# A transformer block with routed spline FFN: second layer norm of y moved to ScalarE, output summed in DRAM from beta rows, x2 and scaled y

## The reference

```python
mod = silu(c) @ wmod                       # sa, ca, ga, sb, cb, gb per sequence
h = layernorm(x) * (1 + ca) + sa
x = x + ga * attention(h)                  # q, k, v, |scores| causal softmax, Wo: this sum is x2
h = layernorm(x) * (1 + cb) + sb
# routed FFN on h
tile_idx = best of 64 signatures (cluster of 8, then 8 in it), scores = h @ sigs.T
comp = tanh(gelu(h @ w1 + b1) @ w2 + b2)
mag  = spline of comp with the tables of tile_idx          # one number per row
y = h + mag * directions[tile_idx] * output_scale
y = (y - mean(y)) / sqrt(var(y) + 1e-5) * norm_gamma + norm_beta
out = x + gb * y
```

## Time and profile before

| | us |
|---|---|
| three runs, median (lowest to highest) | 448.58 (447.64 to 449.85) |
| the profiled execution | 450.27 |
| its span, first to last instruction | 448.4 |
| TensorE, VectorE, ScalarE, GpSimd busy | 398.0, 381.2, 305.8, 32.8 |

### The profile page before, as it was taken

One profiled execution on the slowest core, in us unless ns is written; L12 is line 12 of the kernel. 1 busy time (PEld: TensorE's weight loads), 2 busy tenths in 40 slices (PEclk: granted clock), 3 DMA queues, 4 the chain that ended last, 5 costly groups with the idle time before them and its releaser, 6 DMA issues.

```text
span 448.4 us, 7857 instructions
## 1 busy us (share of the span) xinstructions
PE 398.0 (89%) x2107; PEld 309.7 (69%) x2107; DVE 381.2 (85%) x1464; ACT 305.8 (68%) x670; POOL 32.8 (7%) x77
## 2 busy tenths in 40 slices
PE   8999999999999998999999999999999978947120
PEld 8786776886787787786877687768777765736110
DVE  4785548789989988999889888898889999998996
ACT  1435767886998599769983798478956885755420
POOL 4000061000000011000101001010101010001110
PEclk9999999999999999999999999999999999966555
DMA  7723503033003243430428004432314144007153
GB/s 226 233 57 92 144 5 118 0 119 111 8 2 118 95 94 59 131 96 24 72 93 190 24 2 90 136 97 32 62 57 99 20 70 72 1 1 118 27 75 109
DMA packets 32907, 35.66 MB, mean 80 GB/s; under 512 B 3370, under 2 KB 28448, under 8 KB 32864
## 3 DMA queue, kind: packets, MB, share of 16 engines
q1 hardware_dynamic: 25024, 27.15, 19.6%
q0 software_dynamic: 7536, 7.48, 12.1%
q10 hardware_dynamic: 304, 0.54, 0.4%
HBM read 19.36 MB, written 15.79 MB: 78 GB/s over the span
## 4 chain that ended last, share of the span: by engine, by line
PE 78%; DVE 9%; ACT 7%; issue 5%; DMA 1%; DVEq 0%; ACTq 0%
PE bank L610 14%; PE bank L627 13%; PE bank L587 12%; PE bank L600 12%; PE bank L649 7%; PE bank L618 4%; PE bank L636 3%; PE bank L575 3%; PE bank L689 3%; PE bank L680 2%; DVE y L2316 1%; DVE res L2330 1%; ACT gath L1365 1%; DVE y L2293 1%; ACT xhat L1256 1%
## 5 line engine op out<-in xcount | busy, mean ns | idle before, releaser
L627 PE MATMUL bank<-v,probsT 128*128 128x257 f32 x320 | 79.3, 382 | 2.0 <-ACT probsT L1293 0.9
L610 PE MATMUL bank<-h,g 128*128 128x128 f32 (+3 forms) x256 | 78.6, 434 | 0.0
L627 PEld LDWEIGHTS bank<-v,probsT 128*128 128x128 f32 x320 | 58.1, 190 | 14.7 <-issue 3.7
L600 PE MATMUL bank<-m_ga,h 128*128 128x258 f32 x256 | 65.4, 382 | 2.1 <-ACT onehotT L1359 1.6
L587 PE MATMUL bank<-h,a_sb 128*128 128x512 f32 x128 | 60.0, 594 | 0.0
L600 PEld LDWEIGHTS bank<-m_ga,h 128*128 128x128 f32 x256 | 46.2, 190 | 13.5 <-issue 5.1
L610 PEld LDWEIGHTS bank<-h,g 128*128 128x128 f32 x256 | 42.7, 190 | 16.4 <-issue 9.3
L2032 POOL DMA_DIRECT2D out<-res x14 | 17.9, 1280 | 346.8 <-DVE res L2330 255.1
L1282 ACT ACTIVATE bank<-bank,v 128x128 f32<-128x128 f32 (+1 forms) x64 | 31.8, 498 | 15.7 <-PE bank L610 15.5
L1287 ACT ACTIVATE probs<-probs,negmax 128x128 f32<-128x128 f32 (+1 forms) x64 | 35.8, 562 | 6.3 <-DVE negmax L2145 6.0
L1306 ACT ACTIVATE wide<-x,nmr,rstd 128x256 f32<-128x256 f32 x64 | 35.2, 594 | 4.1 <-DVE nmr L2090 4.1
(11 more groups left out here) (183 smaller groups left out, 792.4 us busy)
## 6 DMA issues: line engine op xcount, KB each, us to landing
x<-in_L_attn_x SPq DMA_DIRECT2D x16, 512.0 KB, 3.9
out<-x SPq DMA_DIRECT2D x14, 512.0 KB, 5.0
out<-res POOLq DMA_DIRECT2D x14, 512.0 KB, 6.3
gb_row<-gate_rows SPq DMA_DIRECT2D x16, 256.0 KB, 3.4
a_row<-gate_rows SPq DMA_DIRECT2D x14, 256.0 KB, 3.6
out<-res SPq DMA_DIRECT2D x2, 512.0 KB, 3.5
wide<-in_L_wmod SPq DMA_DIRECT2D x1, 768.0 KB, 8.2
wide<-in_L_wmod ACTq DMA_DIRECT2D x1, 512.0 KB, 5.8
```

The costliest lines, as they stand in the source:

```text
L600: last = mm(ps[:, 0:VW], h[s][:, c, t * P:(t + 1) * P], m_ga[p % 2][s][:, c, :], start=(c == 0), stop=(c == KC - 1))
L610: last = mm(ps[:, 0:w], g[s][:, c, t * P:(t + 1) * P], h[s][:, c, 0:w], start=(c == 0), stop=(c == KC - 1))
L627: last = mm(ps[:, 0:D + 1], probsT[s][t][:, j * P:(j + 1) * P], v_sb[s][:, j, 0:D + 1], start=(j == 0), stop=(j == t))
```

## The change

- The mean of y comes without reading y. `FS` gets one more column of -1/D (FW = 137), so the mean of h arrives with the scores, `table` holds the mean of each direction, and `spl` gets two more small steps that give `nmu3`.
- The variance: ScalarE squares (y + nmu) with a running sum (`y_sq`, 64 of them). `y_st` is gone, `y_var` is one small instruction.
- Groups 0 to 7: ScalarE normalises y (`yh`, 56 tiles), VectorE multiplies by gb*gamma (`yg`, one instruction for `oa` and `ob`).
- out: SyncE first spreads the row gb*beta over a sequence of out (`beta`, from DRAM to DRAM), GpSimd adds x2 (`ax`) and then the scaled y (`ay`), both by accumulating transfers. y has two buffers.
- `ms` and `base` move from VectorE to GpSimd. `ms(p)` for p > 2 and `base(g)` wait for the first y of a group, group p-2 for ms and g for base.
- Groups 8 and 9 keep `oa`, `base` and `ob`; `send` goes out in halves.
- All banks and the orders of all five queues are new.

```diff
-    FW = NCL + NTILES + H
+    MEAN = NCL + NTILES
+    FW = MEAN + 1 + H
...
+        nmu3, guess3 = ([sb(f"{n}_3{q}", [P, PT]) for q in range(2)] for n in ("nmu", "guess"))
+        y = [sb(f"y{q}", [P, PT, D]) for q in range(2)]
...
@@ sync
-            def xo(g, i):
-                spq.wait_ge(x2_rdy, NT * (before(g) + i + 1))
-                spq.dma_start(out_v[GROUPS[g][i]], x2[p % 2][s][:, :, :]).then_inc(x2_sent[p % 2][s], 16)
+            def beta(g, i):
+                p, s = of_group(g, i)
+                if g == 0:
+                    spq.wait_ge(gb_sent, 16)
+                need(spq, x2_sent[p % 2][s], 16 * (p // 2))
+                rows_ = gate_rows[GROUPS[g][i]:GROUPS[g][i] + 1, 3 * D:4 * D]
+                spq.dma_start(out[GROUPS[g][i]], rows_.broadcast_to([S, D])).then_inc(beta_sent[p % 2][s], 16)
...
@@ scalar
+            def y_sq(g, t):
+                n = NT * before(g)
+                act.wait_ge(nmu_rdy, g + 1)
+                act.wait_ge(y_rdy, n + t + 1)
+                need(act, ln3_var, g)
+                A(gath[:, t, PAR:GW], y[g % 2][:, t, :], ACT.Square, bias=nmu3[g % 2][:, t:t + 1],
+                  accum_out=ln3["sq"][:, t:t + 1]).then_inc(sq_rdy, 1)
             def yh(g, t):
                 act.wait_ge(ln3_ready, g + 1)
-                A(y[:, t, :], y[:, t, :], ACT.Identity, bias=ln3["nmr"][:, t:t + 1],
+                own = y[g % 2][:, t, :]
+                A(own, own, ACT.Identity, bias=ln3["nmr"][:, t:t + 1],
                   scale=ln3["rstd"][:, t:t + 1]).then_inc(yhat_rdy, 1)
...
@@ gpsimd
+            def ms(p, s):
...
+                need(pool, v_done, NT * seq(p - 2, s) + NT)
+                if p > 2:
+                    pool.wait_ge(y_rdy, NT * seq(p - 3, 0) + 1)
+                tt(m_ga[p % 2][s][:, :, 0:D], m_sb[:, :, :],
+                   a_row[p % 2][s][:, 0:D].unsqueeze(1).broadcast_to([P, KC, D]), ALU.mult).then_inc(ms_rdy, 1)
+            def base(g, u):
...
+                pool.wait_ge(y_rdy, NT * before(g) + 1)
+                tt(res[:, o:o + 2, :], x2[p % 2][s][:, t, :],
+                   gb_row[g % 2][u // 2][:, 1:2, :].broadcast_to([P, 2, D]), ALU.add).then_inc(base_rdy, 1)
+            def ax(g, i):
+                (p, s) = of_group(g, i)
+                pool.wait_ge(beta_sent[p % 2][s], 16 * (p // 2 + 1))
+                pool.wait_ge(x2_rdy, NT * (before(g) + i + 1))
+                gp.dma_start(out_v[GROUPS[g][i]], x2[p % 2][s][:, :, :], accum_op=ALU.add).then_inc(x2_sent[p % 2][s], 16)
             def ay(g, i):
-                pool.wait_ge(alone_rdy, NT * (before(g) + i + 1))
+                pool.wait_ge(scaled_rdy, NT * (before(g) + i + 1))
...
@@ vector
-            def y_st(g, t):
-                dve_ln3.mark(v.bn_stats(ln3["st"][:, t, :], y[:, t, :]))
             def y_var(g, i):
-                variance(i, dve_ln3, ln3, slice(0, tiles(g)), ln3_var)
+                dve.wait_ge(sq_rdy, NT * before(g + 1))
+                ts(ln3["var"][:, own], ln3["sq"][:, own], 1.0 / D, EPS, ALU.mult, ALU.add).then_inc(ln3_var, 1)
+            def yg(g, t):
+                dve.wait_ge(yhat_rdy, NT * before(g) + t + 1)
+                own = y[g % 2][:, t, :]
+                tt(own, own, gb_row[g % 2][t // NT][:, 0, :], ALU.mult).then_inc(scaled_rdy, 1)
...
             def y_(g, t):
-                need(dve, alone_rdy, min(NT * before(g), NT * before(g - 1) + t + 1))
+                need(dve, summed[g % 2][t // NT], 16 * len(with_slot(range(g % 2, g, 2), t // NT)))
...
```

More of the change, by code:

```diff
@@ L1959, in _ @@
                 c_ga(9, i)
+            y_gs(8)
+            for i in range(0, 4):
+                y_sq(9, i)
             y_gs(9)
@@ L2727, in _ @@
+            b_x2(2, 1, 0)
+            for i in range(3, 8):
+                clc(2, i)
+            b_ttr(2, 1, 3)
+            b_ri(2, 1, 1)
+            b_x2(2, 1, 1)
+            clc(2, 8)
+            y_var(0, 0)
+            y_nw(0, 0)
+            clc(2, 9)
+            a_st(4, 0, 0)
+            b_st(2, 0, 3)
+            y_nw(0, 1)
+            for i in range(0, 5):
+                clb(2, i)
+            y_nw(0, 2)
             pick(2, 0)
-            b_st(2, 0, 2)
+            y_nw(0, 3)
@@ new lines, in _ @@
+            for i in range(2, 4):
+                clc(4, i)
+            a_nw(5, 1)
+            y_nw(2, 1)
+            a_nw(5, 2)
+            clc(4, 4)
+            b_ri(4, 0, 2)
+            a_nw(5, 3)
+            b_v(4, 1, 2)
+            b_x2(4, 0, 2)
+            for i in range(2, 4):
+                y_nw(2, i)
+            clc(4, 5)
+            for i in range(0, 7):
+                spl(3, i)
+            b_ri(4, 0, 3)
+            b_x2(4, 0, 3)
+            spl(3, 7)
+            clc(4, 6)
@@ new lines, in _ @@
+            y_nw(3, 2)
+            yg(2, 5)
+            b_ri(5, 0, 3)
+            b_x2(5, 0, 3)
+            b_st(5, 0, 1)
+            y_nw(3, 3)
+            yg(2, 6)
+            b_ttr(5, 1, 3)
+            b_ri(5, 1, 0)
+            spl(4, 7)
+            for i in range(2, 5):
+                clb(5, i)
+            b_st(5, 0, 2)
+            b_x2(5, 1, 0)
+            b_ri(5, 1, 1)
+            y_(4, 0)
+            yg(2, 7)
+            y_(4, 1)
+            pick(5, 0)
+            y_(4, 2)
@@ new lines, in _ @@
+            b_v(6, 1, 2)
+            y_nw(4, 1)
+            yg(3, 3)
+            b_x2(6, 0, 1)
+            clc(6, 6)
+            for i in range(0, 6):
+                spl(5, i)
+            yg(3, 4)
+            b_v(6, 1, 3)
+            yg(3, 5)
+            b_ri(6, 0, 2)
+            y_nw(4, 2)
+            spl(5, 6)
+            b_ttr(6, 1, 2)
+            spl(5, 7)
+            b_st(6, 0, 0)
+            yg(3, 6)
+            y_nw(4, 3)
+            b_ri(6, 0, 3)
+            for i in range(2, 4):
+                b_x2(6, 0, i)
@@ new lines, in _ @@
+            b_ri(7, 0, 2)
+            y_nw(5, 3)
+            b_x2(7, 0, 2)
+            pick(7, 1)
+            b_ri(7, 0, 3)
+            b_st(7, 0, 2)
+            b_x2(7, 0, 3)
+            b_st(7, 0, 3)
+            yg(5, 0)
+            c_var(8, 0)
+            for i in range(0, 4):
+                spl(6, i)
+            for i in range(1, 3):
+                c_var(8, i)
+            spl(6, 4)
+            c_var(8, 3)
+            spl(6, 5)
+            b_ttr(7, 1, 0)
+            b_v(7, 1, 2)
@@ L3642, in _ @@
[L3642 to L3646 removed]
+            yg(5, 3)
+            for i in range(7, 10):
+                loc(7, i)
+            for i in range(0, 3):
+                lob(7, i)
+            yg(5, 4)
+            c_b2(7)
+            for i in range(3, 5):
+                lob(7, i)
+            for i in range(0, 2):
+                oh(7, i)
+            for i in range(4, 7):
+                y_(6, i)
+            b_ri(7, 1, 1)
@@ new lines, in _ @@
+            yg(5, 7)
+            for i in range(0, 2):
+                clb(8, i)
+            b_ri(7, 1, 3)
+            b_x2(7, 1, 3)
+            b_st(7, 1, 3)
+            for i in range(0, 3):
+                c_var(9, i)
+            clb(8, 2)
+            c_var(9, 3)
+            for i in range(3, 5):
+                clb(8, i)
+            for i in range(0, 4):
+                spl(7, i)
+            y_var(6, 0)
+            for i in range(0, 4):
+                c_nw(9, i)
+            for i in range(4, 6):
+                spl(7, i)
@@ new lines, in _ @@
+            yg(6, 4)
+            y_var(7, 0)
+            for i in range(7, 10):
+                clc(9, i)
+            for i in range(5, 7):
+                yg(6, i)
+            for i in range(0, 3):
+                clb(9, i)
+            for i in range(0, 3):
+                y_nw(7, i)
+            clb(9, 3)
+            yg(6, 7)
+            clb(9, 4)
+            pick(9, 0)
+            y_nw(7, 3)
+            pick(9, 1)
+            for i in range(0, 4):
+                spl(8, i)
+            c_b2(9)
```

3604 lines of the change are left out of this document (1705 added, 1899 removed), and 16 rows, old and new, of the table BANK.

## The result

| | median (lowest to highest) | runs |
|---|---|---|
| before | 448.87 us (447.64 to 449.85) | 6 |
| after | 452.15 us (450.95 to 452.73) | 6 |

The ratio is 1.0062, 95% interval 1.0037 to 1.0087. The forecast was 436 us, so it missed by 16 us and on the wrong side, and the time lies above its range of 426 to 450. The profiled execution of the changed kernel took 451.87 us, with a span of 449.8.

A forecast was written before the change was run, and what follows sets the result against it. TensorE was taken to bound attention and VectorE's emptying queue the last 56 us. Attention ending at 391 plus a tail of 45.2 gave a span of 436, the median span + 0.2: 436 us, range 426 to 450.

The forecast's parts named there:

- Collisions: GpSimd's 20 products running beside VectorE instructions: taken as 1 us, with up to 26 us possible, 5 in the tail.
- priced back-to-back: VectorE's removed and added tail instructions, counted at their spacing in unbroken runs: net 14.5 us, 50.3 falls to 36.
- density: VectorE's busy share in the tail: 96% before, 86% to 88% forecast, making 37 us of work last 42 us.
- every microsecond taken from VectorE counts: In the last 56 us, taken as VectorE's queue emptying, each microsecond removed there counts until another limit is met.
- the last line of the forecast: Sign of error: a tail over 50 us despite less VectorE work would mean group 9's chain sets it, not the queue.
- VectorE no longer late in 360 to 392: Late attention: TensorE regains some of its lost 10.1 us, so attention ends at 391 instead of 392.4.
- rival 1: ScalarE becomes the bound in attention, its exp, abs and copy links queued behind squares: 458 us, chance 0.13.
- span + 0.2: Step from profiled span to median: the profiled execution lay 1.87 us above its span and 1.69 above the median.
- the square at 0.50 us: ScalarE's new square with a running sum, 64 of them: 0.50 us each, ends 0.41 and 0.61.
- ScalarE's total: ScalarE's busy time in attention, 80 to 389.2 us: 239.8 becomes 283 of 309.2 us, 91%.
- products not late for V_: GpSimd's ms arrive before TensorE's V_ in attention: no loss at the middle value, about 0.2 at 1.84 us per product.
- beta and the accumulating transfers hidden: Spreading beta and adding x2 and y to out by summing transfers: zero cost, 1 to 2 us at the upper end.

The follow-up runs named there:

- e3: The changed kernel without the wait of ms(p) for the first y of group p-2: 454.05 us, ratio 1.0122 to the kernel before.
- e9: The changed kernel with ms of pairs 2 to 7 and the four base back on VectorE, ms of pairs 0 and 1 on GpSimd: 445.28 us.
- e14: The kernel before with VectorE's dependent steps of group 9 set side by side, no work added or removed: 454.19 us, ratio 1.0109.
- e7: The kernel before with the 16 oa and 16 ob of groups 6 and 7 cut to 8 of 256 columns: 444.10 us, ratio 0.9907.
- e13: e9 with the 16 yg of groups 6 and 7 cut to 8 of 256 columns: 444.71 us, ratio 0.9898 to the kernel before.
- e10: e9 with two table loads moved in ScalarE's queue, so c_oht(9,0), c_ga(9) and c_ga(8,0..1) come earlier: 445.75 us.
- e1: The changed kernel with all ms and base products back on VectorE, GpSimd keeping only its transfers: 446.89 us, ratio 0.9958 to the kernel before.
- e2: The changed kernel with ScalarE's 64 squares and 56 normalised tiles cut to 8 of 256 columns: 449.17 us, ratio 1.0008 to the kernel before.
- e8: The kernel before with 64 squares and 56 normalising instructions added on ScalarE, results unread, VectorE keeping all its work: 476.38 us, ratio 1.0624.
- e11: e8 with oa and ob of groups 0 to 7 and all bn_stats of y cut to 8 columns on VectorE: 472.9 us, ratio 1.0559.

## Why the prediction was wrong

1. **Collisions were sized at 1 us; they cost 6.5.** This is the step that turned the sign. The four base in the tail cost 1.0% (1.0062 against 0.9962) and ms of pairs 2 to 7 another 0.45% (0.9962 against 0.9917): 4.5 and 2.0 us. The forecast had the bound (up to 26 us, up to 5 in the tail) and the right rule, and took the low end with the argument that VectorE has 24% free in attention. In the tail the held instructions lay on group 9's steps. The price of one was too low as well: 0.3 to 1.3 us was assumed, up to 2.15 was measured in this kernel, where an issue stood directly ahead of the product. The Trainium skill, "SBUF — State Buffer", Who interferes with whom, says that the first to issue holds the shared ports for its whole instruction and the other blocks. The two-input L2372, begun at 424.38 beside the product of 424.22 to 425.59, ends at 425.63 instead of after 0.19 us, and agrees. L2378, two-input as well, ends with its product too (429.76 and 429.50), but its record begins 0.51 us before the product's, so the records don't show which issued first. The Trainium skill says there too that an instruction outside the two-port modes with one SBUF input is free of this, and the one-input L2478 of e3, 5.24 us beside issues and two products, doesn't settle that, since no run tells its mode.

2. **VectorE's work was priced back-to-back; what stayed was dependent steps.** In the tail before, the durations of the 200 instructions add up to 66.6 us (each group's count by its mean) in 50.7 busy: 15.9 us of overlap. In e9 it is 51.2 in 42.95: 8.3. The durations fell by 15.4 us, the busy time by 7.8. Less the four base (4 x 0.60) that is 40.5 us, not 36. The removed oa, ob and bn_stats were the work between the steps of group 9, and had cost only what they didn't overlap; e14 shows the effect without the change. In 80 to 389.2 us VectorE's busy time fell by 23.3 us (277.47 to 254.20) and not by 42.4. Held instructions are at most 8.6 us of that gap of 19; the rest has the same sign as in the tail, but no run parts it.

3. **The tail isn't one queue.** The forecast divided VectorE's work by a density, its busy share from the last x2 to its last instruction, of 86% to 88%. That density came true: 44.9 of 51.5 us, 87%, in the changed kernel, 91% in e9 (42.95 of 47.35). So the tail's miss in the sum is the work of point 2 and the collisions, not the density. What failed here is the rule behind it, that every microsecond taken from VectorE counts: e7 wins 4.2 us for 7.8 already in the kernel before, e13 some 0.9 for 3.4, with overlapping intervals. That a dependent chain of group 9 through VectorE, ScalarE and TensorE had become equally long is argued and not shown: e10, which moves links of it forward, gains nothing. The chance for that stood in the last line of the forecast only, not among the rivals. Points 2 and 3 together: from the end of the last x2 49.5 us without products on GpSimd (393.8 to 443.3 in e9), 44.2 forecast.

4. **The end of attention: 391 forecast, 393.8 without the products, 396.1 with them** (the end of the last x2, 0.48 us behind its start; 393.8 is the earliest of the four kernels that share these orders, up to 395.7). TensorE was to lose less than its 10.1 us; from 80 us to the last x2 it loses 12.9 (315.66 - 302.74), and 11.5 without products (313.33 - 301.79). The relief of VectorE, 23.3 us of busy time to 389.2, bought nothing. The forecast had "VectorE no longer late in 360 to 392" as its reason, but in the kernel before TensorE's waits of over 0.2 us from 80 to 392 name ScalarE for 9.2 us and VectorE for one of 0.5; only rival 1 looked at them. What ScalarE had itself waited for isn't in these waits. The waits of TensorE from 80 us to 396 us in the changed kernel (engine, line, releaser: us, times, longest):

```profile
PE bank L632 <- ACT gath L1377: 1.6, 1, 1.6
PE bank L641 <- ACT onehotT L1370: 1.4, 1, 1.4
PE bank L632 <- ACT probs L1297: 1.2, 2, 0.7
PE bank L688 <- DVE onehot L2433: 1.0, 1, 1.0
PE bank L601 <- ACT h L1276: 1.0, 1, 1.0
```

All five stand in e1 and e2 as well, with 0.8 to 1.6 us each, so neither the products nor the length of ScalarE's new instructions makes them. The order, the banks and the number of ScalarE's instructions are left; no run tried another order of attention, so the cause of these 2.8 us stays open.

5. **Span to median: 2.15 us.** The forecast took the median as span + 0.2, since the profiled execution of before lay 1.69 us above its median. The changed kernel's lies 0.28 us below, so its median is span + 2.35. That correction was a draw of the spread, not a property of the kernel.

6. **Right:** the square at 0.50 us, ScalarE's total, products not late for V_ (0.7 us once), beta and the accumulating transfers hidden, rival 1 not borne out (ScalarE is at 90%, and e2 brings the last x2 only 0.65 us earlier). But e8 and e11 show how near it was: in the kernel before the same load costs 28 us. Rival 1's own sum leaves out the 3.4 us of transfer behind its 408 + 50.

The sum of the misses: 5.5 (point 1, beyond the 1 us allowed), 5.3 (points 2 and 3), 2.8 (point 4), 2.15 (point 5): 15.75, which is 452.15 less the 436.4 that the forecast's sum gives before rounding. The profiled executions spread by 1 to 2 us, so the shares are good to about that.

## What to carry over

Put no GpSimd arithmetic beside a VectorE chain that sets the end, and none directly behind a GpSimd issue; in the set-up it gained 0.4% here. Price removed VectorE work by what it costs in the gaps of what stays: sum the durations, compare them with the busy time, and ask which overlap goes with it. Before counting relief of a queue in full, cut its work as a trial: here a microsecond of VectorE's work cut from the tail was worth about half of one before the change (e7), and after it about a quarter, with overlapping intervals (e13).

## What the runs showed of the hardware

- VectorE can stand 5.2 us (173.69 to 178.93) for an instruction of 0.4 us or less while GpSimd works through issues and two 128x512 products. Beside a product alone an instruction took 0.3 to 1.1 us more than else, in the changed kernel.
- A ScalarE instruction with a running sum is followed by a read-out record of 0.19 us, and still two of them start 0.50 us apart, as two normalising ones do.
- An accumulating transfer's issue took 1.80 us in the mean for x2 and 1.29 for y, though both carry 512 KB in the same form (22.6 and 18.0 us for 14, overlaps counted once). Why wasn't tested.
